# One edge pass of a graph network: block work of TensorE and ScalarE behind a run's values, and two table loads behind the landed rows

## The reference

```python
h = maximum(layernorm(x), 0)
q, k = (concat(h, query) @ Wq + bq), (concat(h, query) @ Wk + bk)      # 8 heads of 16
v = h @ Wv + bv
scores = sum(q[dst] * (k[src] + relation[edge_type]), -1) / 4           # per edge and head
w = exp(scores - segment_max(scores, dst))
out = segment_sum(w * v[src], dst) / (segment_sum(w, dst) + 1e-8)
x = x + out @ Wo + bo
```

## Time and profile before

| | us |
|---|---|
| median of three runs | 7942.78 (7936.55 to 7952.53) |
| the profiled execution | 7937.73 |
| its span in the profile | 7936.0 |
| the pass of the change | from 1118 to 2856, 1738 us |

### The profile page before, as it was taken

One profiled execution on the slowest core, in us unless ns is written; L12 is line 12 of the kernel. 1 busy time (PEld: TensorE's weight loads), 2 busy tenths in 40 slices (PEclk: granted clock), 3 DMA queues, 4 the chain that ended last, 5 costly groups with the idle time before them and its releaser, 6 DMA issues. The chain is left out here.

```text
span 7936.0 us, 112987 instructions
## 1 busy us (share of the span) xinstructions
PE 2893.9 (36%) x28649; PEld 2358.6 (30%) x28650; DVE 4600.8 (58%) x10704; ACT 1481.2 (19%) x3863; POOL 3660.9 (46%) x4402
## 2 busy tenths in 40 slices
PE   4179633455655532344233431345200000001334
PEld 3168512344545422334223431334200000000122
DVE  9677435566666636677467865677444444443333
ACT  0123100111111121222212222344311111110000
POOL 0155223333332324565445544554466666654555
PEclk9999996666777766676666766667555555555677
DMA  0034223334343523345333443334332222222334
GB/s 21 10 90 107 63 80 95 95 103 104 94 97 86 99 63 70 76 88 76 72 75 80 82 77 68 75 75 79 48 51 51 52 52 53 51 49 61 73 84 81
DMA packets 293996, 576.70 MB, mean 73 GB/s; under 512 B 137262, under 2 KB 182043, under 8 KB 273827
## 3 DMA queue, kind: packets, MB, share of 16 engines
q0 software_dynamic: 113232, 255.82, 21.2%
q1 hardware_dynamic: 142642, 278.18, 11.4%
q10 hardware_dynamic: 38049, 41.86, 1.7%
HBM read 479.10 MB, written 29.32 MB: 64 GB/s over the span
## 5 line engine op out<-in xcount | busy, mean ns | idle before, releaser
L3053 PE MATMUL bank<-tab,oh 128*128 128x136 bf16 x11700 | 894.3, 249 | 654.6 <-PEq L3045 387.2
L3053 PEld LDWEIGHTS bank<-tab,oh 128*128 128x128 bf16 x11700 | 865.0, 111 | 714.6 <-issue 714.5
L1422 PE MATMUL bank<-ident,hid 128*128 128x128 f32 x125 | 55.8, 447 | 2636.6 <-issue 1297.8
L1422 PEld LDWEIGHTS bank<-ident,hid 128*128 128x128 f32 x125 | 22.7, 182 | 2683.4 <-issue 2683.4
L2791 POOL DMA_INDIRECT land_a<-table,idx_a x624 | 665.3, 1066 | 228.4 <-issue 166.4
L2810 POOL DMA_INDIRECT land_r<-table,idx_r x492 | 502.5, 1021 | 214.9 <-issue 149.4
L2901 DVE TENSOR_TENSOR prod<-prod 128x128 f32<-128x128 f32 (+4 forms) x621 | 536.5, 864 | 14.6
L2976 ACT ACTIVATE rows<-bank 128x408 f32<-128x408 f32 x936 | 397.8, 515 | 753.9 <-ACTq L2975 554.9
L2602 PE MATMUL bank<-tab_l,oh_l 128*128 128x128 bf16 x3846 | 404.7, 240 | 210.3 <-issue 103.5
L2887 DVE TENSOR_TENSOR prod<-rows,bank 128x5376 f32<-128x5376 f32 x75 | 431.6, 5755 | 51.5 <-DVEq L2886 39.5
L3312 PE MATMUL bank<-tab_l,oh_l 128*128 128x384 bf16 x1250 | 260.1, 378 | 445.6 <-PEq L3306 333.2
(11 more groups left out here) (512 smaller groups left out, 8558.2 us busy)
## 6 DMA issues: line engine op xcount, KB each, us to landing
loc<-el_loc SPq DMA_DIRECT2D x78, 1088.0 KB
loc_l<-el_loc SPq DMA_DIRECT2D x52, 1088.0 KB
typ_l<-el_typ SPq DMA_DIRECT2D x52, 672.0 KB
rows_r<-land_r SPq DMA_DIRECT2D x123, 272.0 KB
landings_l<-landings_l SPq DMA_DIRECT2D x41, 784.0 KB
attr<-in_edge_attr ACTq DMA_DIRECT2D x75, 343.8 KB
land_a<-table,idx_a POOLq DMA_INDIRECT x936
land_r<-table,idx_r POOLq DMA_INDIRECT x492
```

What stands on the lines that cost most here:

```text
L3053: last = pe.matmul(got[g % full][:, (c - of[0]) * W1:(c - of[0] + 1) * W1], oh[:, o], tab[:, t, x], start=n == 0, stop=n == len(parts) - 1 ...
```

## The change

On TensorE the early keys of run r + 1, its remaining keys and its values now form one unit, and the loop over a block does that unit for the next run; the first run's unit stands ahead of the loops. So `to_conv` and `node_update` come behind the values of run r + 1, not between the early and the remaining keys. On ScalarE `exps(0)` of the next run is taken at the end of `runs_of_block`, and `to_conv`, `node_update`, `keep_sums` and the next `take_landed` follow it. On SP each `load_loc(r)` but the first waits until the first gathers of run r have landed (`got_a_l0`). At the end of the pass there is one unit more than there are runs, and VectorE gives and takes the signals for its twelve key banks and twelve value banks.

```diff
-                    def load_loc(r):
+                    def load_loc(r, ahead=True):
+                        if ahead:
+                            sp.wait_ge(s("got_a_l0"), r * (16 * FIRST) + 16 * FIRST)
                         sp.wait_ge(s("loc_free"), 1)
...
-                    load_loc(0)
+                    load_loc(0, ahead=False)
...
                     finish()
+                    dve.sem_inc(s("shifted"), 1)
+                    dve.wait_ge(s("exped"), 1)
+                    dve.sem_inc(s("exped"), -1)
+                    for n in range(len(key_groups) + len(value_groups)):
+                        dve.wait_ge(s(f"bank_full{n % len(banks)}"), 1)
+                        dve.sem_inc(s(f"bank_full{n % len(banks)}"), -1)
+                        if n < len(key_groups) + len(value_groups) - len(banks):
+                            dve.sem_inc(s(f"bank_free{n % len(banks)}"), 1)
                     for name, n in [("agg_free", 1), ("land_r_free", 1), ("rows_r_free", 1), ("land_a_free", 2)]:
...
-                    for n in range(AHEAD):
-                        dve.wait_ge(s(f"bank_full{n}"), 1)
-                        dve.sem_inc(s(f"bank_full{n}"), -1)
...
                         with act.Fori(r0, r1) as r:
-                            exps(0)
                             turns = turns_of_overflow(act, r)
                             take_landed(r + 1)
                             with act.Fori(0, turns):
                                 exps(MC - MORE)
+                            exps(0)
...
+                    exps(0)
                     runs_of_block(0)
...
                         with pe.Fori(r0, r1):
+                            early_keys()
                             keys(groups_of_keys[AHEAD:])
                             values()
-                            early_keys()
...
                     early_keys([0])
+                    keys(groups_of_keys[AHEAD:])
+                    values()
                     block_of(0)
```

## The result

The changed kernel took 8081.56 us (median of 4 runs, 8079.77 to 8095.24) against 7939.66 us: ratio 1.0188, 95% interval 1.0165 to 1.0211. The forecast was 7907 us, so both the sign and the range missed.

A forecast was written before the change was run, and what follows sets the result against it. It took a cross-engine chain ending in the loads' new wait to bound one-turn runs. Terms - 7 - 38 - 12 + 21 = - 36 us took 7937.7 to 7902, median 7907; range 7825 to 8050, the forecast's own 7825 to 7927.

The forecast's parts named there:

- the term for what the gathers do to TensorE: TensorE's values near the mark (start of scaling totals): gathers and backlog add 2.5 us, bounded by 0 and 7.9.
- the chain's 54.5: One-turn runs: linked waits across engines from mark to mark sum to 53.6 us, or 55.4 with loads at 14.
- VectorE's own 45.5 us: VectorE's work in a one-turn period, without its waits: about 57.5 - 12 = 45.5 us.
- The chain to the loads: One-turn runs: values, block work, landed groups, gathers and landing precede the loads, issued some 40 us after the mark.
- while the loads move, the gathers hardly do: DMA queues: gathers barely advance beside the loads of positions and types, 60 packets against 304.
- A rule against it: DMA queues: overflow gathers wait until loads are through, against the skill's round robin; 60 packets against 304.
- Two-turn runs: Periods with two overflow turns: taken as 63.1 us, 6.4 less than 69.5, six times 38 us.
- held-back early keys: Rival: gathers delay TensorE's early keys; one-turn period 60.6, two-turn runs lose 3 us, + 94 us, 8037 us; chance 0.23.
- The removed wait: VectorE before the first remaining keys bank: 4.14 us and hand-overs behind it go, some 4 to 8 us a run.
- The end: End of the pass: one unit too many and ScalarE's last block work behind it add 21 us, exposed.
- The last one: Rival: gathers flow beside loads, TensorE slow until overflow gathers end at 49; period 67, 8098 us; chance 0.10.
- wait does not bind: Rival: loads or landings come sooner than summed, so VectorE's work counts; - 203 us, 7740 us; chance 0.10.

The follow-up runs named there:

- e3: Changed kernel with TensorE itself waiting for the landed rows in place of ScalarE's `keys_in`, loads' wait kept; with gaps 7933.17 us against 7923.24 before, ratio 1.0011.
- e6: Kernel before the change, with TensorE itself waiting for the landed rows; gap-free 7359.80 us against 7362.14 before, ratio 0.9999.
- e8: Changed kernel run again unedited, in a gap-free group; 7691.86 us against 7362.14 for the kernel before, ratio 1.0450.
- e1: Changed kernel without the loads' new wait, so the new order alone; with gaps 8040.99 us against 7923.24 before, ratio 1.0156.
- e13: Changed kernel without the loads' new wait, so the new order alone; gap-free 7426.88 us against 7359.00 before, ratio 1.0089.
- e2: Kernel before the change with only the loads' new wait added, old order kept; with gaps 7977.07 us against 7923.24, ratio 1.0068.

## Why the prediction was wrong

**The step that failed** is the term for what the gathers do to TensorE: "I take 2.5, nearer the lower end, as six banks stand full". The banks don't stand full. `keys_in` waits behind the block work, the landed groups are the first two of TensorE's six, and the gathers start right behind them, so only these two are computed by then; in e3 all six are. The wait is not 2.5 us but 16.71, above the upper bound of 7.9 that I had drawn from the earlier trace rows, and it is not before the values near the mark, where the term had put it (0.3 us in all fourteen one-turn runs), but before the early keys. In the sum's terms the period of 65.2 us is 10.7 above the chain's 54.5: the loads' part is 4.9 (below), and the late keys' is 5.8, where 2.5 stood. I had listed "TensorE's group 0 waits" among what is queued behind `keys_in` and priced it only as a link of GpSimd's chain, not as a delay of VectorE's keys. e3 shows its price: 9.4 us a one-turn run.

**The earlier trace rows was read a little low.** Its 347.6 us belong to 24 runs, so it is 14.5 us a run and not 13.9. VectorE's own 45.5 us were close all the same: e6, where it hardly waits, has a period of 44.1 us.

**The chain to the loads was right, and their length was not.** Block work 13.9 us (14.3), loop entry 2.3 (1.9), loads issued at mark + 38.8 (39.4). The loads were put at 12.2 to 14 us; in e8 they need 18. The step "while the loads move, the gathers hardly do" misread, and "A rule against it" rests on the same reading: the first gather of that window was issued at 2064.37, so they flowed for the last third only. From 2064 to 2069 us the queues of before are

```profile
q1 hardware_dynamic: 111, 0.85, 80.9%
q0 software_dynamic: 60, 0.20, 17.1%
```

so the gathers move beside the loads there too, once they are issued. With 18 us the chain is 39.4 + 18 + 2.0 = 59.4, which is the gap-free period of 59.0. With gaps it is hidden, by 6 us, behind the late keys.

**Two-turn runs: + 4.1 us, not - 6.4.** The order alone gives 69.0 (e1), the own wait changes nothing (e3), the loads' wait adds 4.6. Its way, in e1 without the wait (SP and GpSimd, mark 1704.90):

```profile
1763.16 0.53 SPq L2179 DMA_DIRECT2D landings_l<-landings_l  x1
...
1767.17 0.19 POOL L2235 COPY idx_r_l<-run_now_l 128x8 int32 x1 [6.45 <-POOLq L2234]
```

and in after (mark 1722.32, the next 1794.96):

```profile
1791.35 0.53 SPq L2181 DMA_DIRECT2D landings_l<-landings_l  x1
...
1795.37 0.19 POOL L2237 COPY idx_r_l<-run_now_l 128x8 int32 x1 [11.84 <-POOLq L2236]
```

In both the first turn's gathers end about 11 us behind the copy of their list, which stands at mark + 45.1 in e1 and at mark + 50.5 in after. In e1 their rows are copied out at mark + 58.3. In after the loads are issued at mark + 53.2 on top of them, and the copy comes at mark + 69.0. The second turn's gathers then begin at the next mark in place of 6 us ahead of it and lie on the values. VectorE waits 6.2 us a two-turn run for these (2.9 in e1) and 4.5 before the overflow turns' values (3.4 in e1), which together is 4.4 of the 4.6 us. That the loads' packets hold the rows back is argued from e8's queues, not shown by a run of its own. The rival "held-back early keys" had the sign and nearly the size (3 us a run), but put these gathers at mark + 8 to 18, on ScalarE's block work; they lie at mark + 1.4 to 11.1, on the values.

**The removed wait** of 4.14 us is gone: after has the six remaining banks in one go in its one-turn runs. **The end** was put at 21 us and measured 25, all of it the order's (e1, e13); e2 has 1 us.

**The rivals.** The last one (slow stretch up to the overflow gathers' end, period 67, 8098 us, chance 0.10) comes nearest: 65.2 us and 8082. It put the end of the gathers at 50 and 17.1 us behind it; the run shown has 46.4 and 18.8. It reached that by loads and gathers moving side by side, which they do, but e3 has the same gathers and loads and 55.8 us, so what decided is one that it did not name, the late landed groups. The rival "wait does not bind" holds with gaps in its name alone: the wait is hidden, but not because loads or landings came sooner, and VectorE's own work did not become the bound.

**What stays open.** Why TensorE shows gaps beside the gathers in some groups of runs and none in others, with the same program; no run told it. The late landed groups are what makes the gaps fall on keys that VectorE waits for; what makes the gaps is not known. Nor was it traced why the later passes of after take 15 us less.

## What to carry to other kernels

Before moving a block of work on an engine, list every word that this engine passes on for others; a word that only says "landed" is better awaited by its user, and here, with gaps, it decided between 1.0188 and 1.0011. An added wait that does not show in the profile can still cost: with gaps it costs 0.65% (e2), where VectorE stands before the types no longer than it did (20.4 us in the pass, 20.2 in before), and in the gap-free runs it becomes the bound. Price a slow engine by what stands computed ahead of it when it slows, not by the longest wait seen so far.

## What the runs showed of the hardware that was not expected

- The same kernel took 7923, 7362, 7918 and 7359 us (medians of the kernel before) in four groups of runs. The difference seen in the traces is TensorE's gaps between matmuls while gathers flow (the changed kernel in both cases): 42 matmuls in 20 us at a mean granted clock of 0.61, against 313 in 21 us at 1.00. A clock at its lower level (1.2 GHz) would only double the durations, so it doesn't account for the gaps.
- It is not shown to be the chip: a group with gaps and one without are both listed under chip 13.
- The price of a change depends on it, also in order: with gaps the order costs 1.6% and the wait 0.65%; gap-free 0.9% and 1.8%.
- 304 packets of the loads and 306 of the gathers pass in the same 18 us (e8): with seven gathers issued beside them, the three loads take 18 us up to the types, in place of 12 with four issued beside them (before).
